# Keys' weights staged as fp32 on the tokens' queue and cast on chip, with the last attention chunk and the passage to the feed-forward part reordered

## The reference

```python
x = x + layernorm(attn(layernorm(x), Wq, bq, Wk, bk, Wv, bv))
x = x + layernorm(ffn(layernorm(x), w_gate, w_up, w_down))

# attn: q, k, v = h @ W.T + b, in 64 blocks of 64 tokens. The first and the last block attend
# to all keys; every other block to the first block, its own and its two neighbours, the last block
# ffn:  h = silu(x @ wg.T) * (x @ wu.T);  return h @ wd.T      # int weights times 1/127
```

## Time and profile before

| | us |
|---|---|
| time, median of 3 runs | 1537.97 (1537.17 to 1540.72) |
| the profiled execution's own time | 1537.16 |
| its span on the slowest core (core 1) | 1536.1 |
| spans of the eight cores | 1524.9 to 1536.1 |
| PE busy in it | 1496.2 (97%) |
| DVE, ACT, POOL busy | 660.0, 452.5, 262.4 |

### The profile page before, as it was taken

The page is one execution under the profiler, slowest core; times in us unless marked ns, Lnnn a source line. Parts: engine busy times, 40 slices in busy tenths (PEclk is TensorE's granted clock), DMA queues, the critical chain, the costliest instruction groups (busy, mean ns, idle before and its releaser), DMA issues.

```text
span 1536.1 us, 26835 instructions; the slowest of 8 cores (1524.9 to 1536.1 us)
## 1 busy us (share of the span) xinstructions
PE 1496.2 (97%) x10032; PEld 723.2 (47%) x10032; DVE 660.0 (43%) x1264; ACT 452.5 (29%) x587; POOL 262.4 (17%) x576
## 2 busy tenths in 40 slices
PE   3999999999999999999999999999999999999998
PEld 2445555555555544444444444444444444444443
DVE  5164454554634354244344344435424434433113
ACT  2266555555556611111111111111101111111111
POOL 4022232332323531010010010011001001000001
PEclk9999999999999999999999999999999999999999
DMA  9655677878766876323333223423322423312002
GB/s 212 117 106 109 133 139 161 170 158 173 131 129 114 298 253 206 94 90 96 90 117 92 67 97 95 110 83 110 89 77 90 96 90 116 96 49 96 1 1 96
DMA packets 130494, 178.43 MB, mean 116 GB/s; under 512 B 65472, under 2 KB 97216, under 8 KB 128960
## 3 DMA queue, kind: packets, MB, share of 16 engines
q1 hardware_dynamic: 110912, 99.11, 26.3%
q0 software_dynamic: 19024, 77.08, 19.4%
q10 hardware_dynamic: 432, 0.53, 0.2%
HBM read 136.85 MB, written 69.21 MB: 134 GB/s over the span
## 4 chain that ended last, share of the span: by engine, by line
PE 96%; DMA 2%; issue 1%; ACT 1%; DVE 1%; POOL 0%; DVEq 0%; SPq 0%; ACTq 0%; POOLq 0%
PE ps L662 21%; PE ps L652 21%; PE ps L712 21%; PE ps L292 15%; PE ps L322 8%; PE ps L375 4%; PE ps L433 3%; PE ps L429 1%; PE ps L436 1%; DMA xx<-x_in 1%; DMA attn_d<-ast 1%; PE ps L620 1%; DMA xst<-x_in 1%; ACT pb L389 0%; PE ps L262 0%
## 5 line engine op out<-in xcount | busy, mean ns | idle before, releaser
L662 PE MATMUL ps<-x2T,wu_sb 128*128 128x512 bf16 x1536 | 363.7, 380 | 2.9 <-DVE hsw L668 2.9
L652 PE MATMUL ps<-x2T,wg_sb 128*128 128x512 bf16 x1536 | 363.6, 380 | 0.0
L712 PE MATMUL ps<-wd_sb,hsw 128*128 128x512 bf16 x1488 | 322.5, 379 | 0.0
L668 DVE TENSOR_TENSOR hsw<-ps,sgb 128x512 bf16<-128x512 f32 x192 | 132.6, 691 | 313.0 <-PE ps L662 313.0
L666 ACT ACTIVATE sgb<-ps 128x512 bf16<-128x512 f32 x192 | 114.6, 597 | 514.0 <-PE ps L652 498.1
L662 PEld LDWEIGHTS ps<-x2T,wu_sb 128*128 128x128 bf16 x1536 | 150.3, 98 | 184.9 <-issue 4.5
L652 PEld LDWEIGHTS ps<-x2T,wg_sb 128*128 128x128 bf16 x1536 | 150.4, 98 | 181.7 <-issue 1.6
L712 PEld LDWEIGHTS ps<-wd_sb,hsw 128*128 128x128 bf16 x1488 | 145.6, 98 | 175.6
L173 POOL TENSOR_TENSOR small<-small 128x1 f32<-128x1 f32 x127 | 75.5, 594 | 766.8 <-DVE small L171 766.8
L389 ACT ACTIVATE pb<-ps 128x1024 bf16<-128x1024 f32 (+2 forms) x128 | 117.5, 957 | 131.0 <-PE ps L375 131.0
L380 ACT ACTIVATE pb<-ps 128x1024 bf16<-128x1024 f32 x128 | 124.1, 1022 | 49.8 <-PE ps L375 49.8
(11 more groups left out here) (78 smaller groups left out, 1076.8 us busy)
## 6 DMA issues: line engine op xcount, KB each, us to landing
xx<-x_in SPq DMA_DIRECT2D x34, 512.0 KB, 5.5
attn<-attn_d SPq DMA_DIRECT2D x32, 512.0 KB, 3.8
x_d<-xx POOLq DMA_DIRECT2D x32, 512.0 KB, 6.7
x1r<-x_d SPq DMA_DIRECT2D x32, 512.0 KB, 3.4
out<-x1r POOLq DMA_DIRECT2D x31, 512.0 KB, 3.0
xst<-x_in SPq DMA_DIRECT2D x29, 512.0 KB, 6.1
attn_d<-ast SPq DMA_DIRECT2D x58, 256.0 KB, 3.6
wgb_d<-wgT POOLq DMA_DIRECT2D x24, 256.0 KB, 5.1
```

The costliest lines, as they stand in the source:

```text
L652: mm = te.matmul(gp[:, p2], wg_sb[:, hc * 1024 + dc * 128:hc * 1024 + (dc + 1) * 128], xTn[:, dc * 512:(dc + 1) * 512], start=(dc == 0), s ...
L662: mm = te.matmul(upp[:, p2], wu_sb[:, hc * 1024 + dc * 128:hc * 1024 + (dc + 1) * 128], xTn[:, dc * 512:(dc + 1) * 512], start=(dc == 0), ...
L668: tok["hu", g] = DV.sig(dv.tensor_tensor(hsw[:, hc * 512:(hc + 1) * 512], upp[:, p2], sgb[:, p2], ALU.mult))
L712: mm = te.matmul(ys[:, half * 512:(half + 1) * 512], hsw[:, hc * 512 + tt * 128:hc * 512 + (tt + 1) * 128], wd_sb[:, hc * DM + half * 512: ...
```

## The change

**Start.** The keys' weights no longer come by POOL's casting queue. `wst_load(u)` fetches one unit as fp32 (512 KB) on SP's queue into one of four staging areas, and `wk_cast(u)` writes it as bf16, on ACT for units 0 and 1, on DVE for the other six. A staging area is loaded again only after its cast. Unit 0's weights stand behind tile 3 on the queue, units 1 to 4 behind tile 7. Tiles 4 and 5 no longer wait for tiles 1 and 2. `bv`'s transfer moves from ACT's queue to the end of this row on SP's. POOL issues the V and Q loads after unit 6's weights have landed. `ln1_b(3)` stands ahead of `ln1_a(4)`. Only `k_group(0, 0)` stands between the transposes: `k_group(0, 1)` stands behind that of tile 6, and the rest behind that of tile 7, for chunks 0 and 1 by turns.

**Last chunk.** `q_group` of the next unit is split after four matmuls, and piece 2 of the scores stands in the gap.

**Passage.** `gate(1)` and its Silu stand ahead of `pv(7, 7)`, `gate(2)` behind it. The writing of tile 0's attention, `tile0_out`, stands behind `up(3)`.

```diff
-    d_wk = [Dma(nc, "d_wk%d" % i) for i in range(4)]
+    d_ws = [Dma(nc, "d_ws%d" % i) for i in range(4)]
+    def wst_load(u):
+        SY.need(tok.get(("wk", u - 4)))
+        tok["wst", u] = d_ws[u % 4].sig(sy.dma_start(wst_at(u), wk_d[u]))
     for t in range(4):
         x_load(t)
+    wst_load(0)
     for t in (4, 5):
-        SY.need(tok["x", t - 3])
         x_load(t)
...
+    def wk_cast(u):
+        out = wk_sb[:, u * 1024:(u + 1) * 1024]
+        if u < 2:
+            AC.need(tok["wst", u])
+            tok["wk", u] = AC.sig(ac.activation(out, wst_at(u), AF.Identity))
+        else:
+            DV.need(tok["wst", u])
+            tok["wk", u] = DV.sig(dv.tensor_copy(out, wst_at(u)))
...
-    tok["bv"] = d_bv.sig(ac.dma_start(bv_rep[:], bv_d.to_broadcast([128, DM])))
...
+    def ln_pe(t):
+        ln1_a(t)
+        ln1_b(t - 1)
+        xT_pe(t - 1)
+    ln1_a(0)
+    for t in range(1, 4):
+        ln_pe(t)
+        if t == 2:
+            wk_cast(0)
+    ln1_b(3)
+    xT_pe(3)
+    x_load(6)
+    x_load(7)
+    k_group(0, 0)
+    for u in range(1, 5):
+        wst_load(u)
+    ln1_a(4)
+    for t in range(5, 8):
+        ln_pe(t)
+    ln1_b(7)
+    wk_cast(1)
+    k_group(0, 1)
+    xT_pe(7)
+    wst_load(5)
+    for u in (2, 3):
+        wk_cast(u)
+        wst_load(u + 4)
+    tok["bv"] = d_bv.sig(sy.dma_start(bv_rep[:], bv_d.to_broadcast([128, DM])))
+    x_load(8)
+    for u in range(4, NU):
+        wk_cast(u)
+    PO.need(tok["wst", 6])
+    for n in range(2):
+        wv_load(n)
+    for i in range(4):
+        wq_load(i)
-    for u in range(5):
+    for u in (0, 1):
         k_group(1, u)
-    for c in (0, 1):
-        for u in range(5, NU):
+    for u in range(2, NU):
+        for c in (0, 1):
             k_group(c, u)
...
+        if few and c:
+            q_group(*slots[n + 1], lambda: scores(c, u, 2, 0))
+            scores(c, u, 3, 1)
...
     gate(0)
+    silu(0)
+    gate(1)
+    silu(1)
     pv(7, 7)
-    gate(1)
-    DV.need(tok["g", 7, 7])
-    for i in range(2):
-        tok["gdone"] = to_attn(...)
+    gate(2)
     up(0)
     up(1)
...
             if g >= 2:
                 up(g)
+            if g == 3:
+                tile0_out()
```

More of the change, by code:

```diff
@@ L129, in build_nc @@
     qb = at("qb", PQ + 4 * PW, 2 * 512, BF16)
+    wst = at("wst", TOP, 4 * 1024, F32)
     gacc = at("gacc", TOP + 8192, VW, F32)
@@ L286, in q_buf, with qk_group @@
         return qb[:, o:o + 512]
-    def qk_group(c, u, name, w_sb):
+    def qk_group(c, u, name, w_sb, between=None):
         b, bank = rot_bank()
-        TE.need(tok[name, u // 2], *(tok["xT", 4 * c + j] for j in range(4)))
+        TE.need(tok[name, u], *(tok["xT", 4 * c + j] for j in range(4)))
         for dc in range(8):
+            if dc == 4 and between is not None:
+                between()
             mm = te.matmul(bank, w_sb[:, u * 1024 + dc * 128:u * 1024 + (dc + 1) * 128],
@@ L304, in k_group, with q_group @@
             kt[:, o:o + 512], bank, AF.Identity, bias=bk[:, u:u + 1], scale=1.0))
-    def q_group(c, u):
-        b, bank, t = qk_group(c, u, "wq", wq_sb)
+    def q_group(c, u, between=None):
+        b, bank, t = qk_group(c, u, "wq", wq_sb, between)
         tok["qmm", c] = t
@@ L512, in gate_up_load @@
         tok["wf", i] = ffn_load(i, wu_sb, wub_d, d_wf)
-    w_turn = {0: ((wk_load, 0),), 1: ((wk_load, 1),), 2: ((wk_load, 2),), 3: ((wk_load, 3),),
-              4: ((wv_load, 0),), 5: ((wv_load, 1),), 6: ((wq_load, 0), (wq_load, 1)),
-              7: ((wq_load, 2), (wq_load, 3))}
-    for t in range(9):
-        for load, i in w_turn.get(t, ()):
-            load(i)
-        if t == 1:
-            ln1_b(0)
-        if t < 8:
-            ln1_a(t)
-        if t >= 2:
-            ln1_b(t - 1)
-        if t >= 1:
-            xT_pe(t - 1)
-        if t >= 4:
-            k_group(0, t - 4)
+    def ln_pe(t):
[34 more added lines that the diff above has]
+        wq_load(i)
     DV.need(t_small)
     tok["bqs"] = DV.sig(dv.tensor_scalar(bqs, bqs, QSCALE, None, ALU.mult))
-    for u in range(5):
+    for u in (0, 1):
         k_group(1, u)
-    for c in (0, 1):
-        for u in range(5, NU):
+    for u in range(2, NU):
+        for c in (0, 1):
             k_group(c, u)
@@ L546, in build_nc @@
         more = c + 1 < NCH
-        def band_scores():
-            scores(c, u, 2, 0)
-            scores(c, u, 3, 1)
         scores(c, u, 0, 0)
         scores(c, u, 1, 1)
-        few = c in (0, NCH - 1) and n + 1 < len(slots)
         if more and c > 0:
             k_group(c + 1, u)
-        if n + 1 < len(slots):
+        few = c in (0, NCH - 1) and n + 1 < len(slots)
+        if few and c:
+            q_group(*slots[n + 1], lambda: scores(c, u, 2, 0))
+            scores(c, u, 3, 1)
+        elif n + 1 < len(slots):
             q_group(*slots[n + 1])
-        if few:
-            band_scores()
+            if few:
+                scores(c, u, 2, 0)
+                scores(c, u, 3, 1)
         if n >= 1:
@@ L654, in gate, with silu @@
         tok["gate", g] = TE.sig(mm)
+    def silu(g):
+        p2 = slice((g % 2) * 512, (g % 2 + 1) * 512)
+        AC.need(tok["gate", g], tok.get(("hu", g - 2)))
+        tok["sg", g] = AC.sig(ac.activation(sgb[:, p2], gp[:, p2], AF.Silu, scale=DQ))
     def up(g):
@@ L664, in up @@
         tok["gu", n] = t_u = TE.sig(mm)
-        AC.need(tok["gate", g], tok.get(("hu", g - 2)))
-        tok["sg", g] = AC.sig(ac.activation(sgb[:, p2], gp[:, p2], AF.Silu, scale=DQ))
+        if g >= 2:
+            silu(g)
         DV.need(tok["sg", g], t_u)
@@ L688, in build_nc @@
             g = NHC * n + hc
+            if g >= 3:
+                gate(g)
             if g >= 2:
-                gate(g)
                 up(g)
+            if g == 3:
+                tile0_out()
             i, step = 4 * (n + 1) + hc // 6, hc % 6
```

22 lines of the change are left out of this document (11 added, 11 removed).

## The result

| | before | after |
|---|---|---|
| median time, us | 1537.75 | 1541.6 |
| ratio, with its 95% interval | | 1.0021 (1.0012 to 1.0029) |
| the profiled execution's own time | 1537.16 | 1538.97 |
| its span on the slowest core | 1536.1 (core 1) | 1537.8 (core 3) |
| mean span of the eight cores | 1531.8 | 1533.7 |

A forecast was written before the change was run, and what follows sets the result against it. PE was taken as the bound, busy 1496.2 of 1536.1 us. On core 1, 1536.1 + 0.8 - 1.7 - 0.5 - 1.0 - 4.6 = 1529.1; a chance wait made it 1530.5, and 1.06 around the span 1531.6 us, range 1527 to 1537.

The forecast's parts named there:

- The start's cost: Start to the value groups: +0.8 us on core 1 (60.7 against 59.89), between -0.6 and +4.5; +4.4 on core 5.
- 20 us of slack: Passage: SP's loads behind the writing of tile 0 have 20 us of slack, so nothing new is late.
- the cores end close together: Last step of the sum: a chance wait on one of eight cores sets the slowest, at 1530.5 us.
- The mark of 60.7 us on all cores: Start: first value group on PE at 60.7 us, from tile 0's statistics at 5.5 plus 55.2 us.
- tile 0 lands as late as now: Rival at the start: tile 0 at 7.99 us on odd cores, core 1 +3.3 us, time 1534; chance 0.15.
- Late landings: Rival at the start: SP's queue no faster alone, tiles or weights late, time 1537.5 to 1541; chance 0.13.
- the wait under `gate(1)`: Passage: the 1.0 us wait for POOL's clearing ahead of `pv(7, 7)` is covered by `gate(1)`: -1.0 us.
- the stall on six cores of eight: Passage: PE's 2.9 us wait for `hu` and the 1.7 us at half clock behind it both go: -4.6 us.
- 7 x (0.35 - 0.10) = 1.7: Last chunk: seven units lose the 0.35 us Exp wait, each paying 0.10 for one more switch: -1.7 us, between 0 and -2.4.
- The term of -0.5: Last chunk: the first wait for POOL's clearing (0.6 us), which stood behind the late Exps, goes: -0.5 us.
- one, at 3 us: One of eight cores meets a chance wait for a tile's transposing transfer: 2.0 us, with the clock about 3.
- the rival with 3 us of the gains missing: Last chunk and passage: the Exp ring does not loosen and the passage finds another wait, 1534.6 us; chance 0.12.

The follow-up runs named there:

- late groups: Kernel before with only the change's order of key groups on PE, weights still by POOL's casting queue: ratio 1.0035 (1.0022 to 1.0048).
- version with all the parts: Kernel before with the start of early groups, the change's last chunk, and its passage without SP's wait for tile 0's attention: ratio 0.9940, median 1531.18 us.
- early groups: Kernel before with the change's start transfers, but key groups of units 0 to 3 between the transposes; last chunk and passage as before: ratio 0.9962 (0.9948 to 0.9975).
- casts apart: Changed kernel with the feed-forward weights' casting transfers issued in units 0 to 3 and 7 of a chunk, none in 4 to 6: ratio 1.0028 (1.0011 to 1.0044).
- the last version: Version with all the parts, plus the attention loop's tiles one unit earlier: ratio 0.9944 (0.9925 to 0.9963).

## Why the prediction was wrong, point by point

**Where the miss lies.** Three steps failed. The start's cost was set against the mark of core 1 alone, the write that was moved was given 20 us of slack, and the slowest core was put 1 us above the mean. On core 1, for which the sum was made, 1529.1 was forecast and 1535.6 measured. Of these 6.5 us the passage has 3.9 (88.31 where 89.97 - 5.6 was forecast), the start 1.7 (62.38 for 60.7) and the loop with the last chunk 0.9 (465.85 for 467.13 - 2.2). The other part is the last step of the sum, "the cores end close together", which put the slowest core at 1530.5, some 1 us above the mean that the sum gives. In ten executions of after the mean of the cores was 1535.3 us and the slowest stood 4.8 above it, and in 64 of the kernel before, timed beside the experiments, 5.4 above it. So this step had the distance wrong by some 4 us, whatever the change did.

**The start, right as a time.** The mark of 60.7 us on all cores came at 59.97 to 63.44, mean 61.52. `k_group(0, 1)` was forecast 24.8 us behind the first statistics, at half speed. On core 1 it stands 24.8 us behind them (32.51 less 7.73). On core 3 it stands 27.1 us behind them, since tile 1 landed late (8.95, which the sum had no term for, 2.3 us), and it took 3.36. The cast took 1.05 on ACT (L233) where 1.0 was put. From tile 0's first statistics to the values it is 54.7 us on core 1, where 55.2 was forecast. But tile 0 itself was forecast at 5.5 us on core 1 and came at 7.73, as late as before (7.99), although `bv` and the casting queue were gone: this term was 2.2 us too small, and the rival "tile 0 lands as late as now" came true there. On the other odd cores it did not (4.80, 4.95 and 4.87 on cores 3, 5 and 7). "Late landings" is out: DVE waited for none of the tiles 2 to 7, and PE for no cast after the first two.

**The start, wrong in what it is compared with.** The first step that failed is the one that fixed the start's cost by core 1: +0.8, against a mark of 59.89 that was taken as core 1's own. The four profiles with the old start show that the mark of a core moves from execution to execution. Timelines of the kernel with only the passage changed, cores 0 and 1:

```profile
57.83 4.48 PE L324 MATMUL ps<-wv_sb,xT 128*128 128x512 bf16 x20
...
55.51 6.85 PE L324 MATMUL ps<-wv_sb,xT 128*128 128x512 bf16 x31
```

The same program start gave 53.91 and 59.89 before. The mean of the eight hardly moves (56.42, 55.85, 56.62, 56.85). The sum had its own number for this: the start loses "3.3 us on core 1 and 6 on core 0" from the arrival of tile 0. It should have set 60.7 against the mean of 56.4, +4.3. With the last chunk's -2.2, the wait under `gate(1)` (-1.0) and the stall on six cores of eight (-4.6 x 6/8), the mean would have fallen by 2.4 us, 0.15%: near no change. Measured were +5.1 for the start and +1.9 for the mean span. The spread of before was read as a fixed handicap of core 1 that the change could remove. Most of it is the luck of one execution: in the profile core 1 ends 11.2 us behind core 0, and in 20 to 23 executions of the same kernel on each of three chips 2.2, 1.9 and 0.3 us behind it on the mean. The change put all eight cores at the late end. Tile 0 of core 1 arrived at 6.7 to 8.0 us in all four profiles, but at 5.06 in the late groups, which load it the same way, so even that is not the core's own.

**The last chunk, mechanism right, size wrong.** The Exp waits and ACT's gap went. The term was 7 x (0.35 - 0.10) = 1.7 and measured 7 x 0.18 = 1.3: a unit of core 1 gained 0.07 us less than put. The term of -0.5 for POOL's wait ahead of `pv(7, 6)` became +0.5: PE arrives there earlier, POOL is done, and DVE's adding-up of `pv(7, 5)` is next, 1.1 us. The sum had followed this product's wait for POOL and not the one for DVE behind it. Values to `gate(0)` fell by 0.8 to 1.3 us on undisturbed cores, where -2.2 was forecast, and by 0.5 on the mean. The waits without a semaphore that came with the split group had no term at all. That the wait ahead of `pv(7, 7)` would go under `gate(1)` came true.

**The passage, right on the stall and wrong on what comes next.** The product wait at 541 us is gone on all eight cores. "Nothing new is late: SP's loads behind the writing of tile 0 have 20 us of slack" is the sentence that failed. The divisions move 6.6 us later (538.07 to 544.67), POOL's burst of weight loads (545.31 to 553.36) falls on the writing of tile 0, and SP holds the next load for it: 555.88 against 546.96. The next tile's statistics read this load, and DVE is free for them at 557.99, 29.8 us behind `gate(0)` (528.23). The load took 9.6 us from its issue to them here (555.88 to 565.52), so by this one landing it had to leave 20.1 us behind `gate(0)`. Before, it left 19.9 us behind it (546.96 less 527.02). The slack behind the old issue was about 0.2 us, not 20: the step left out how long the load lands in this traffic and that a product stands behind the statistics on DVE. The -5.6 of this stage (-1.0 and -4.6) became -1.7 on core 1 (89.97 to 88.31), -2.6 on the mean. Without SP's wait it is -3.7 on the mean, which includes the two cores that had no stall to lose, -5.5 on the mean of the other six, and -5.9 on core 1: the size of the term was right, and the new wait took it back.

**The chance waits, underrated.** The forecast had one, at 3 us, on one of eight. The changed kernel and the tries show them from 0.6 to 6.5 us on PE. A core with one of 6.5 us and 1.9 us without a semaphore lost 12 us (477.92 against 466.0). The two groups right behind the longer wait took 3.57 and 2.54 us instead of 1.89, 2.3 of the rest. That the closer start makes the slowest core worse is not borne out: it stood 4.8 us above the mean after and 5.4 before. Whether the new transfers make the waits more frequent is open: among the eight profiles with them 1, 4, 2, 3, 0, 1, 0, 1 of the eight cores waited for `xT` on PE, and among the five with the old transfers 1, 1, 1, 1, 0. The cores' marks lie 2.5 to 4.2 us apart in the first and 3.0 to 6.0 us in the second, so being in phase hardly tells them apart. And the version with all the parts has none in its profile, and the same with earlier tiles has losses on six cores, most of them without such a wait. This stays open, and so does what holds PE without a semaphore.

**Transfers of 512 KB.** The transfers of after brought 3.84 MB from 10 to 22 us on core 3, in 512 KB transfers on one queue, and DVE got its tiles in time. By the Trainium skill, DMA: Bandwidth & Descriptors, section Rules for kernel authors, a transfer should be at least 1 MiB for full bandwidth. The sum left this rule out as not binding, and nothing in the trace speaks against that: the queue kept the 16 engines at 99.2%. No run here tries transfers of 1 MiB. DMA queues of after on core 3, 10 to 22 us: packets, MB, share of 16 engines:

```profile
q1 hardware_dynamic: 1057, 3.84, 99.2%
```

**Chances.** 0.09 was given to slower. Its case was late landings, which did not come. Of the rival with 3 us of the gains missing (0.12) the half came in which the passage finds another wait. The case that came, the start at its forecast time on cores that were not late before, stood in the text only as core 5's sum.

## What to carry to other kernels

Take a core's lateness in one profile as an execution's luck until a second profile shows it, and set a new stage time against the mean of the cores, not against the slowest. Take the distance from the mean to the slowest from many executions. A group that could run between transposes and is moved behind them costs PE its time and can cost it its full speed, however early its operands come: the new transfers paid 3.6 us here with the groups in the gaps and 1.4 with the groups behind them. For a moved write, look for whoever waits in the same queue for its landing, and count from its new time, in the traffic of that time.

## What the runs showed of the hardware

- One queue alone moved 3.70 MB in 12 us (10 to 22 us, core 1 of after), with the 16 engines busy throughout. Before, three queues moved 2.66 MB there by the profile's count, 0.88 of it on the casting queue. But this count takes a casting transfer by the bf16 bytes that it writes (512 KB for `wk_load`, which reads two units of 512 KB of fp32). By the bytes read it is 3.5 MB, so one queue is hardly faster than three. What is new for the tokens is their place: one unit of weights is asked for ahead of tile 7 in the change, and all eight before it.
- A cast from fp32 to bf16 of 128x1024 takes 1.05 us on ACT and 0.69 on DVE.
- A second group of eight matmuls that starts 11 us behind the first, with three sets of transposes between, runs near half speed again (3.36 us on core 3 of after); with one set of transposes between them it takes 1.89 to 2.77 (early groups).
- A transposing transfer of one tile, issued in the attention loop, lands in 11.0 us on core 4 and 15.0 on core 3 of after (medians of two, from 285 to 315 us), and in some 20 us on core 7 of the kernel without SP's wait, issued at 293.56.
- PE can stand inside a run of matmuls with no semaphore to wait for: 7.63 us before 180.52 with a transposing transfer late on the same core (casts apart), 2.3 to 4.0 us on four cores at one place of the program (the last version), 0.3 to 2.8 us in the last chunk of the kernels with the split group. In the kernel with only the last chunk changed the places are the same on every core that stands there and 9.2 to 9.3 us apart (509.42, 518.66 and, in a `gate`, 527.99 on core 0). What PE then waits for the profile doesn't say.
